# A four-layer graph network on one core: the first layer's gather in three fp32r terms, with earlier first norm, query staging and last norm

## What is computed

```
h = relu(layernorm(x)); x = x + (h - (adj @ h) * (d1 + 1)) @ W + bias          # L0
h = relu(layernorm(x)); x = x + sigmoid(gate_a * (attn @ (h @ W_sa)) + gate_b * (adj @ (h @ W_gc) + b_gc))   # L1
h = relu(layernorm(x)); twice: Wh, Ws = split(h @ W)                            # L2a, L2b
                        h = leaky_relu((softmax(Wh @ Ws.T) * adj) @ Wh + h)
x = x + h
h = relu(layernorm(x)); two steps (A0, A1): A = softmax over the nucleus (0.9) of (Xa W1 W2 (Xa W3).T)       # L3
                        Xf = Rf @ Xf; Xb = Rb @ Xb; Xa = A @ Xa; Z += Xf U1 + Xb U2 + Xa U3
x = x + layernorm(h + Z) * gamma + beta
```

## Time and profile before

| | |
|---|---|
| time, median of 3 runs | 1161.16 us (1160.06 to 1163.42) |
| time of the profiled execution | 1161.47 us |
| its span in the trace | 1159.6 us |
| mean granted PE clock | 0.915 of 2.4 GHz |
| busy: PE, PEld, DVE, ACT, POOL | 928.5, 766.6, 757.3, 512.6, 39.0 us |

### The profile page before, as it was taken

How to read it: one execution, slowest core, us unless ns; L and a number is a source line. 1 busy time by engine, 2 the same in 40 slices (tenths; PEclk the granted TensorE clock), 3 DMA queues, 4 the chain that set the end, 5 groups by cost and what they waited for, 6 DMA issues and landing times.

```text
span 1159.6 us, 13986 instructions
## 1 busy us (share of the span) xinstructions
PE 928.5 (80%) x4807; PEld 766.6 (66%) x4807; DVE 757.3 (65%) x1288; ACT 512.6 (44%) x886; POOL 39.0 (3%) x101
## 2 busy tenths in 40 slices
PE   3998799958999789996779598979699299713883
...
DMA packets 42895, 32.67 MB, mean 28 GB/s; under 512 B 3218, under 2 KB 40796, under 8 KB 42844
## 3 DMA queue, kind: packets, MB, share of 16 engines
...
HBM read 30.63 MB, written 1.39 MB: 28 GB/s over the span
## 4 chain that ended last, share of the span: by engine, by line
PE 19%; DVE 14%; issue 13%; ACT 6%; DVEq 0%; ACTq 0%; POOL 0%; POOLq 0%
PE out L808 6%; ACT u_rows_a L599 4%; PE scores L923 3%; DVE e_strip L1518 2%; PE turned_ps L941 2%; DVE small L1301 2%; DVE is_tie L1471 1%; DVE run L1402 1%; DVE e_strip L1522 1%; PE scores L837 1%; PE scores L848 1%; DVE tmp L1393 1%; PE turned_ps L848 1%; PE scores L718 1%; PE turned_ps L923 1%
## 5 line engine op out<-in xcount | busy, mean ns | idle before, releaser
L599 ACT ACTIVATE u_rows_a<-e_rows,small 128x1354 f32<-128x1354 f32 x104 | 146.6, 1411 | 19.4 <-DVE small L1340 19.4
L808 PE MATMUL out<-h_rows,adj_strip 128*128 128x256 f32 x484 | 108.8, 382 | 0.0
L779 PE MATMUL out<-feat,adj_t 128*128 128x256 f32 (+1 forms) x484 | 107.5, 380 | 1.5 <-DVE x_rows L1116 1.5
L779 PEld LDWEIGHTS out<-feat,adj_t 128*128 128x128 f32 x484 | 91.4, 189 | 15.6 <-DVE x_rows L1116 1.9
L808 PEld LDWEIGHTS out<-h_rows,adj_strip 128*128 128x128 f32 x484 | 91.3, 192 | 11.7
L923 PE MATMUL scores<-feat_fb,adj_strip 128*128 128x512 f32 x154 | 73.0, 633 | 17.0 <-ACT feat_fb L624 13.5
L1346 DVE SCALAR_TENSOR_TENSOR tmp<-e_rows,small 128x1354 f32<-128x1354 f32 x52 | 84.5, 1625 | 0.0
L708 PE MATMUL turned_ps<-ident,tmp 128*128 128x128 f32 x132 | 30.8, 332 | 55.9 <-ACT tmp L433 39.0
L923 PEld LDWEIGHTS scores<-feat_fb,adj_strip 128*128 128x128 f32 x154 | 31.3, 205 | 56.0 <-issue 38.4
L616 ACT ACTIVATE e_strip<-e_rows,small 128x1354 f32 (+1 forms) x22 | 31.3, 1421 | 74.8 <-DVE small L1553 34.0
L1346 DVE SCALAR_TENSOR_TENSOR kept_tile<-e_rows,small 128x1354 f32<-128x1354 f32 x39 | 63.4, 1626 | 0.0
...
## 6 DMA issues: line engine op xcount, KB each, us to landing
...
```

The costliest lines, as they stand in the source:

```text
L599: act.activation(out2[:, (k % 2) * N:(k % 2 + 1) * N], E[:, t, :], [ACT.Relu, ACT.Sign][k % 2], bias=nudged[:, t:t + 1], accum_out=[relu_s ...
L779: ins = pe.matmul(bank[:, 0:n], AT[:, j, cols(t)], features[:, j, 0:n], start=(j == 0), stop=(j == NT - 1))
L808: ins = pe.matmul(OUT[b][:, 0:D], ADJ[:, b, j, :], H[:, j, :], start=(j == 0), stop=(j == NT - 1))
```

## The change

Three engines' programs change at the start, POOL's four waits, and two engines' programs at the end.

1. **First norm.** DVE aggregates and makes the variance right behind the statistics, ACT takes the root ahead of splitting the weights, DVE finishes the norm ahead of its part of the split.
2. **First gather.** `gather_l0` is replaced by the three-term gather that L2a uses. ACT rounds a strip of `AT` (`strip_l0`), DVE makes the rest (`strip_rest_l0`), with tile 0's strip put into the projection's last turns and each later one as soon as the gather two tiles before it is done. `FH` and `FL` take the place of `F1`, which costs DVE one more 256-wide subtraction for a tile of the projection. The column sums move from DVE to ACT.
3. **Query staging.** POOL's first copies wait for 2 tiles of the projection instead of 11.
4. **Last norm.** It is made in two groups (`END`: tiles 0-7 and 8-10), the first inside the gather's loop.

```
@@ tables @@
+END = [(0, PIECES[1][1]), (PIECES[2][0], NT)]
-STR = {name: NT * k for k, name in enumerate(["L2a", "L2b", "A0", "A1"])}
+STR = {name: NT * k for k, name in enumerate(["L0", "L2a", "L2b", "A0", "A1"])}
@@ gpsimd: staging the queries, the same two lines for A0 and A1 @@
             for name in ("L2a", "L2b"):
-                pool.wait_ge(proj_read, PJ[name] + NT)
-                pool.wait_ge(proj_hi, PJ[name] + NT)
+                pool.wait_ge(proj_read, PJ[name] + 2)
+                pool.wait_ge(proj_hi, PJ[name] + 2)
                 pipeline(pool, (0, q_l2(SCO[name])))
@@ scalar @@
-            split_w("L0", WH[:, :, 0:2 * D], raw[:, :, 0:2 * D])
+            def strip_l0(t, b):
+                wait(act, gathered, GA["L0"] + t - 1)
+                act.activation(SH[:, 1 - b, :, :], AT[:, :, cols(t)], ACT.Copy).then_inc(strip_hi, 1)
+                if not isinstance(t, int) or t >= 1:
+                    act.wait_ge(col_sums, t)
+                act.activation(expt[0], AT[:, bass.ds(t, 1), :], ACT.Copy,
+                               accum_out=colsum[:, bass.ds(t, 1)]).then_inc(col_sums, 1)
+            def first_strip_l0(t, r):
+                if isinstance(t, int) and t == NT - 1:
+                    act.wait_ge(ld_adj, 16 * NT)
+                    strip_l0(0, 0)
             for loaded in ld_x:
                 act.wait_ge(loaded, 16)
-            root("L0")
+            act.wait_ge(var_ready, NORM["L0"])
+            act.activation(std[:, :], var[:, :], ACT.Sqrt).then_inc(std_ready, 1)
+            split_w("L0", WH[:, :, 0:2 * D], raw[:, :, 0:2 * D])
+            act.wait_ge(norm_ready, NORM["L0"])
             act.wait_ge(w_lo, WPREP["L0"])
-            project_rows(PJ["L0"], stage_norm(PJ["L0"]), copy_part(lambda t: F1[:, bass.ds(t, 1), 0:D], 0, D, D))
+            project_rows(PJ["L0"], stage_norm(PJ["L0"]), copy_part(lambda t: FH[:, bass.ds(t, 1), 0:D], 0, D, D),
+                         before=[(3, first_strip_l0)])
             act.wait_ge(projected, PJ["L0"] + NT)
+            strip_l0(1, 1)
             split_w("L1", WH[:, :, 0:D + 6 + D], raw[:, :, 0:D + 6 + D])
             act.activation(WrH[:, :, :], wlr[:, :, 0:1].broadcast_to([P, KB, P]), ACT.Copy).then_inc(w_hi, 1)
+            for t in range(2, NT):
+                strip_l0(t, t % 2)
+            act.wait_ge(gathered, GA["L0"] + NT)
...
-            act.wait_ge(gathered, GA["L0"] + NT)
-            act.wait_ge(var_ready, NORM["end"])
-            act.activation(std[:, :], var[:, :], ACT.Sqrt).then_inc(std_ready, 1)
-            act.wait_ge(norm_ready, NORM["end"])
             def last(t):
                 act.activation(Y[:, bass.ds(t, 1), :], Y[:, bass.ds(t, 1), :], ACT.Identity,
                                bias=nmr[:, bass.ds(t, 1)], scale=rstd[:, bass.ds(t, 1)]).then_inc(fin_a, 1)
-            each_tile(act, last)
+            for g, (t0, t1) in enumerate(END):
+                act.wait_ge(var_ready, NORM["end"] + g)
+                act.activation(std[:, t0:t1], var[:, t0:t1], ACT.Sqrt).then_inc(std_ready, 1)
+                act.wait_ge(norm_ready, NORM["end"] + g)
+                for t in range(t0, t1):
+                    last(t)
@@ tensor @@
-            def gather(name, *groups):
-                def step(t, b):
+            def gather(name, *groups, swap=False):
+                def step(t, place):
+                    b = 1 - place if swap else place
                     wait(pe, strip_hi, STR[name] + t + 1)
                     wait(pe, strip_lo, STR[name] + t + 1)
                     wait(pe, gather_read, GA[name] + t - 1)
                     for c0, fh, fl, n in groups:
                         for m, (left, right) in enumerate([(SH, fh), (SL, fh), (SH, fl)]):
                             for j in range(NT):
-                                ins = pe.matmul(OUT[b][:, c0:c0 + n], left[:, b, j, :], right[:, j, 0:n],
+                                ins = pe.matmul(OUT[place][:, c0:c0 + n], left[:, b, j, :], right[:, j, 0:n],
                                                 start=(m == 0 and j == 0), stop=(m == 2 and j == NT - 1))
                     ins.then_inc(gathered, 1)
...
-            pipeline(pe, (0, gather_l0), peel=NT)
+            pipeline(pe, (0, gather("L0", one, swap=True)))
@@ vector @@
+            norm_open()
...
+            norm_close("L0")
             split_w("L0", WL[:, :, 0:2 * D], raw[:, :, 0:2 * D], WH[:, :, 0:2 * D])
-            norm_stats("L0")
             link0 = chain(dve_tail, 1)
             def evac_l0(t, r):
                 b = r % 2
+                lo(row(FL, t), pbank[b][0][:, D:2 * D], row(FH, t))
                 link0(t, 1, dve.tensor_tensor(row(X, t), row(X, t), pbank[b][0][:, 0:D], ALU.add))
                 return dve.tensor_tensor(row(X, t), row(X, t), bcast[:, :], ALU.add)
-            project_rows(PJ["L0"], evac_l0)
+            def strip_rest_l0(t, b):
+                wait(dve, strip_hi, STR["L0"] + t + 1)
+                wait(dve, gathered, GA["L0"] + t - 1)
+                lo(SL[:, 1 - b, :, :], AT[:, :, cols(t)], SH[:, 1 - b, :, :]).then_inc(strip_lo, 1)
+            def first_rest_l0(t, r):
+                if isinstance(t, int) and t == NT - 1:
+                    dve.wait_ge(ld_adj, 16 * NT)
+                    strip_rest_l0(0, 0)
+            pipeline(dve, (2, turn(PJ["L0"])), (3, first_rest_l0), (4, evac(PJ["L0"], evac_l0)), peel=7, ring=RT)
+            strip_rest_l0(1, 1)
             dve.wait_ge(proj_read, PJ["L0"] + NT)
...
-            def sum_column(t, b):
-                dve.tensor_reduce(one(colsum, t), AT[:, bass.ds(t, 1), :], AX.X, ALU.add).then_inc(col_sums, 1)
-            dve.wait_ge(ld_adj, 16 * NT)
-            pipeline(dve, (0, sum_column), (0, read(GA["L0"], read_l0)))
+            read_tile_l0 = read(GA["L0"], read_l0)
+            for t in range(NT):
+                if t + 2 < NT:
+                    strip_rest_l0(t + 2, t % 2)
+                read_tile_l0(t, t % 2)
...
+                def end_norm(g):
+                    t0, t1 = END[g]
+                    dve.wait_ge(gather_read, GA["A1"] + t1)
+                    for t in range(t0, t1):
+                        ins = dve.bn_aggr(mv[:, t, :], stats[:, t, :])
+                    ins.then_inc(end_step, 1)
+                    dve.wait_ge(end_step, 4 * g + 1)
+                    dve.tensor_scalar(var[:, t0:t1], mv[:, t0:t1, 1], LN_EPS, None, ALU.add).then_inc(var_ready, 1)
+                    dve.wait_ge(std_ready, NORM["end"] + g)
+                    dve.reciprocal(rstd[:, t0:t1], std[:, t0:t1]).then_inc(end_step, 1)
+                    dve.wait_ge(end_step, 4 * g + 2)
+                    dve.scalar_tensor_tensor(out=nmr[:, t0:t1], in0=mv[:, t0:t1, 0], scalar=-1.0, in1=rstd[:, t0:t1],
+                                             op0=ALU.mult, op1=ALU.mult).then_inc(norm_ready, 1)
+                def times_gamma(k):
+                    t0, t1 = PIECES[k]
+                    dve.wait_ge(fin_a, t1)
+                    dve.tensor_tensor(Y[:, t0:t1, :], Y[:, t0:t1, :],
+                                      gam[:, :].rearrange("p (a d) -> p a d", a=1).broadcast_to([P, t1 - t0, D]),
+                                      ALU.mult).then_inc(end_step, 1)
+                def plus_x(k, made):
+                    t0, t1 = PIECES[k]
+                    dve.wait_ge(end_step, made)
+                    dve.tensor_tensor(Y[:, t0:t1, :], Y[:, t0:t1, :], X[:, t0:t1, :], ALU.add).then_inc(fin, 1)
+                def finish_rows(t, b):
+                    if t == NT - 4:
+                        dve.wait_ge(ld_late, 32)
+                        dve.wait_ge(x_beta, 1)
+                        end_norm(0)
+                    elif t == NT - 3:
+                        times_gamma(0)
+                        plus_x(0, 3)
+                        times_gamma(1)
+                    elif t == NT - 2:
+                        end_norm(1)
+                        plus_x(1, 4)
+                        times_gamma(2)
+                        plus_x(2, 7)
+                ends = [(3, finish_rows)] if name == "A1" else []
...
-            norm_stats("end")
-            dve.wait_ge(ld_late, 32)
-            dve.wait_ge(x_beta, 1)
-            for t0, t1 in PIECES:
-                dve.wait_ge(fin_a, t1)
-                then(dve.tensor_tensor(Y[:, t0:t1, :], Y[:, t0:t1, :],
-                                       gam[:, :].rearrange("p (a d) -> p a d", a=1).broadcast_to([P, t1 - t0, D]),
-                                       ALU.mult))
-                dve.tensor_tensor(Y[:, t0:t1, :], Y[:, t0:t1, :], X[:, t0:t1, :], ALU.add).then_inc(fin, 1)
```

18 lines of the change are left out of this document (10 added, 8 removed).

## The result

The changed kernel takes 1150.55 us in the median (1149.56 to 1152.57), the kernel before 1162.29 beside it: a ratio of 0.9903, 95% interval 0.9879 to 0.9927. The forecast was 1143.2 with a range to 1149.5. The sign was right; of 18 us forecast, 11 to 12 came. The profiled execution took 1151.3 us.

The account below looks back on a forecast made before the run. It took PE as busy for 80% of the span and DVE 65%, with separate bounds at each edit. 1161.5 - 7.3 (first norm, gather) + 1.5 (clock) - 3.8 (staging) - 2.7 (clock) - 6.0 (last norm) = 1143.2 us, range 1138.5 to 1149.5.

Parts of the forecast that it names:

- First norm: At the start: staging begins at about 14.2 instead of 16.92, 2.7 us earlier, with the weights' split now last.
- no drain: Behind the first table load: no 1.38 us drain on top; the rival with the drain gave 1144.6, chance 2%.
- of the 2.7 gained, 1.35 is left: At the first gather's start, with tile 0's strip made in the projection: 38.65 instead of 39.99.
- Gather (a): In the first projection: DVE's extra subtraction costs 0; if it binds, 0.1 a tile, 1 us.
- (c): In the first gather: tile 2's strip comes late, so PE starts tile 2 0.95 us late, once.
- (d): The first gather's steady state: about 4.2 us a tile from tile 3 on, against 4.76 before.
- the term at the last read: First norm and gather together, at the first gather's last read: 7.3 us earlier, 5.8 with the +1.5 of (e).
- (e): At the first gather: PE's clock slow behind a 2.8 us idle time, costing up to 2.7; taken as +1.5.
- Query staging: At the first scores of L2a, L2b, A0 and A1: 0.9 to 1.0 us saved each, 3.8 in all.
- under the 2.29 that left the clock alone: At L2a and L2b: PE's idle time falls to 2.2, so one of two half-clock stretches goes, 2.7 us saved.
- the clock stays slow: Rival: the slow clock stays at L2a and L2b, giving 1145.9, up to 1147.4; chance 25%.
- Last norm: At the end: the two-group norm ends the kernel at 1148.55 instead of 1154.59, 6.0 us saved.

Follow-up runs that it names:

- w_norm: The kernel before with the first norm's edit alone and idle matmuls on PE ahead of its first rows; ratio 0.9966 to the kernel before.
- x_warm: The changed kernel with 34 idle identity matmuls on PE ahead of the first staged tile; ratio 0.9869 to the kernel before.
- x_bias: The changed kernel with layer 0's bias addition moved from DVE to POOL; ratio 0.9856 to the kernel before.
- x_nofl: The changed kernel without DVE's extra subtraction in the first projection, the features' rest set to zero; ratio 0.9868 to the kernel before.
- x_swap: The changed kernel with the two branch bodies of A1 in the other order in DVE's program, tied one first; ratio 0.9877 to the kernel before.
- e_query: The kernel before with only POOL's earlier query staging at L2a, L2b, A0 and A1; ratio 0.9975 to the kernel before, 2.9 us faster.

## Why the prediction was too low, by its own steps

- **First norm**: right in its working, 2.90 for 2.7, the split last, no drain. The step that failed carries it on: "of the 2.7 gained, 1.35 is left". None was (40.41 against 39.99). PE was taken at full clock in the projection; it was slow until 21 us before and after, so that an earlier start bought slow time. That took 1.2 of the 2.90 by the second tile, and the pace of the next point 1.0 more by the ninth; the strip itself cost less than forecast (5.78 us from ACT's read of the ninth tile to the gather, where the forecast had 32.6 to 38.65, 6.05). Shown by w_norm and x_warm.
- **Gather (a)**: "I take 0" for DVE's extra subtraction was wrong; the allowance of 1 us was in the range only. DVE's four operations take 1.62 with their overlap, not "about 1.5", and a tile took 1.81 instead of 1.64. x_bias, with the clock rising at the same time, starts the gather 1.5 to 2.2 earlier, x_nofl 2.4, part of which is the clock's.
- **(c), (d)**: the pace was 4.10 for 4.2, and tile 2 began 4.18 behind tile 1, without the 0.95 lost. This made up for the late start, so that the term at the last read was nearly right (5.55 for 5.8) by two errors.
- **(e)**: +1.5 came (40.41 to 45.95 are 5.54 for a tile of 4.1), but by luck: it was reasoned from a wait of 2.8 us, the wait was 2.18, and behind 2.19 in x_swap nothing was slow.
- **Query staging**: 1.0 at each start came (idle 2.22, 2.22, 1.09, 1.60). The step "under the 2.29 that left the clock alone", -2.7, failed: a wait of 2.22 us still came with a stretch of 3.4 us at 0.50 at both, half of the 6.8 before, and none went (at L2a kernels with the old wait have 3.4 as well); what that gave was returned in other slow stretches, in e_query what A0 and A1 gave as well. The rival "the clock stays slow" named this, but not that more would be lost elsewhere.
- **Last norm**: 6.2 for 6.0, right step by step.
- **Missing from the sum**: 2.2 us at the tied branch, since the change moved its target in DVE's program (shown), and some 4.6 of slow stretches that came or grew at L1, ahead of A1 and in A1's second half. That the first and the last of these are slow stretches is in the rows above; from A0's start to A1's the clock records add up to 44.3 us at 0.50, before to 40.9; why they fall as they do from one start to another stays open.
